# A gated delta-rule layer with experts on one Trainium2 core: solving the right sides twice in place of refining the inverse

## What is computed

```python
mixed = silu(causal_conv4(hidden @ Wqkv.T + bqkv))   # q, k: 8 heads of 128; v: 16 heads of 128
q, k = l2norm(q) * 128 ** -0.5, l2norm(k)            # each used by two value heads
def step(state, inp):                                # state: 16 heads x 128 x 128
    q_t, k_t, v_t, g_t, b_t = inp
    state = state * exp(g_t)
    delta = (v_t - k_t @ state) * b_t
    state = state + outer(k_t, delta)
    return state, q_t @ state
core = rmsnorm(outs) * norm_w * silu(z)
x = x + layernorm(core @ Wout.T + bout)
```

## Time and profile before

| | |
|---|---|
| median of 3 runs | 3361.04 us (3360.9 to 3364.18) |
| span of the profiled execution | 3361.6 us |
| TensorE busy | 3184.6 us, 95% |
| VectorE busy | 2731.3 us, 81% |
| ScalarE busy | 2411.1 us, 72% |
| GpSimd busy | 2147.3 us, 64% |
| DMA queue of the kernel | 15.9% of 16 engines |

### The profile page before, as it was taken

How to read it: one execution, slowest core, us unless ns; L and a number is a source line. 1 busy time by engine, 2 the same in 40 slices (tenths; PEclk the granted TensorE clock), 3 DMA queues, 4 the chain that set the end, 5 groups by cost and what they waited for, 6 DMA issues and landing times.

```text
span 3361.6 us, 77100 instructions
## 1 busy us (share of the span) xinstructions
PE 3184.6 (95%) x23968; PEld 2828.4 (84%) x23968; DVE 2731.3 (81%) x8720; ACT 2411.1 (72%) x5922; POOL 2147.3 (64%) x5380
## 2 busy tenths in 40 slices
PE   4999999999999999999999999999999999999996
PEld 3888888888888888888888888888888888888885
DVE  4788888888888888888888888888888888888874
ACT  3777777777777777777777777777777777777762
POOL 3766666666666666666666666666666666666660
PEclk8999999999999999999999999999999999999997
DMA  4111111111111111111111111111111111111110
GB/s 182 43 40 38 44 40 35 45 41 38 39 45 35 39 47 38 36 45 38 38 45 41 36 37 46 38 39 47 37 35 45 41 38 42 43 35 39 47 36 11
DMA packets 424113, 144.75 MB, mean 43 GB/s; under 512 B 211168, under 2 KB 421664, under 8 KB 423200
## 3 DMA queue, kind: packets, MB, share of 16 engines
q1 hardware_dynamic: 423712, 139.83, 15.9%
HBM read 93.11 MB, written 46.66 MB: 42 GB/s over the span
## 4 chain that ended last, share of the span: by engine, by line
PE 66%; ACT 14%; DVE 5%; issue 5%; POOL 5%; DMA 4%; SPq 0%; ACTq 0%; DVEq 0%; POOLq 0%
PE bF L474 8%; PE bB L648 6%; PE bQ L547 5%; ACT L850 4%; PE bXT L560 4%; PE bB L733 3%; PE bB L720 3%; PE bS L615 3%; PE bD L630 3%; PE bS L623 3%; PE bF L485 3%; PE bS L607 3%; PE bF L487 3%; PE bD L608 2%; PE bX L570 2%
## 5 line engine op out<-in xcount | busy, mean ns | idle before, releaser
L1151 DVE SCALAR_TENSOR_TENSOR Y<-bF,Cv,Y 128x127 f32<-128x127 f32 (+2 forms) x3072 | 852.2, 339 | 8.3 <-ACT Y L867 3.4
L474 PE MATMUL bF<-XnT,Wqkv 128*128 128x128 f32 x4096 | 530.9, 277 | 0.5 <-ACT XnT L986 0.5
L474 PEld LDWEIGHTS bF<-XnT,Wqkv 128*128 128x128 f32 x4096 | 504.4, 193 | 9.3 <-issue 1.8
L867 ACT ACTIVATE Y<-bF,Cv 128x128 f32<-128x128 f32 x1024 | 383.4, 455 | 102.5 <-PE bF L474 102.5
L937 ACT ACTIVATE XiT<-bXT 128x512 fp32r<-128x512 f32 x384 | 229.0, 596 | 298.0 <-PE bXT L560 293.4
L1590 POOL TENSOR_TENSOR Tp<-Tp 32x64 f32<-32x64 f32 (+2 forms) x768 | 362.1, 472 | 60.2
L1194 DVE TENSOR_TENSOR Qi<-bQ,Cf 128x512 fp32r<-128x512 f32 x384 | 262.8, 684 | 98.1 <-PE bQ L547 97.0
L850 ACT ACT_TABLE_LOAD x257 | 329.7, 1283 | 5.4 <-PEq L1674 0.7
L560 PEld LDWEIGHTS bXT<-Qi,Xi 128*128 128x128 f32 x1536 | 221.8, 191 | 118.0 <-issue 88.8
L560 PE MATMUL bXT<-Qi,Xi 128*128 128x128 f32 x1536 | 298.7, 317 | 14.3 <-DVE Qi L1194 2.5
L1583 POOL TENSOR_TENSOR Tp<-Yb,Tm 32x64 f32<-32x64 f32 (+1 forms) x384 | 276.0, 719 | 30.1
(11 more groups left out here) (234 smaller groups left out, 9269.8 us busy)
## 6 DMA issues: line engine op xcount, KB each, us to landing
DL<-Ln SPq DMA_DIRECT2D x128, 256.0 KB, 2.2
XiT<-DX SPq DMA_DIRECT2D x128, 256.0 KB, 2.8
Xi<-DX SPq DMA_DIRECT2D x128, 256.0 KB, 3.2
DX<-Yb SPq DMA_DIRECT2D x256, 32.0 KB, 1.9
...
Cb<-DL SPq DMA_DIRECT2D x128, 32.0 KB, 1.9
...
```

What stands on the lines that cost most here:

```text
L474: last = mm(bank[:, i, :], Wqkv[:, k, c:c + P], XnT[:, k, :], start=(k == 0), stop=(k == KT - 1))
L867: last = op(Y[:, tile, :], bank[:, i, :], ACT.Identity, scale=c[:, TAPS - 1:TAPS], bias=c[:, TAPS:TAPS + 1])
L1151: last = stt(y, bank[:, i, 0:P - shift], Cv[:, g * TILES + tile, n:n + 1], y, ALU.mult, ALU.add)
```

## The change

- The inverse drops the identity product, the third `invert_xt`, `turned`, the fourth mask, the NegR product and the copy into Tt. It gains a third `invert_x`, which ScalarE copies into a new buffer XF in fp32r. XF is used transposed.
- GpSimd subtracts the identity from Ln after the triangle has gone to DRAM (`minus_one`); the first mask has -1 on its diagonal in place of 1.
- The right sides are solved by XF in fp32r (`solve`, from R rounded to Rr by ScalarE), the solution Z goes through Ln in full fp32 (`residual`), VectorE adds R (`left_over`), and `correct` multiplies what is left by XF and adds it to the first solution in bS. ScalarE copies the sum to Z again (`corrected`).
- The state stage runs once for four heads in place of twice for two. R, Z, Qg and Kd double in size; Vs, Kn, AT and Ln are kept for 3 items (`live`), which adds waits ahead of their writers.
- The Xi and XiT loads wait for the last `invert_q` and `invert_x` in place of `correct`. The load of Xr is moved behind them in SyncE's queue.
- The loop over 30 chunks is written out without a loop instruction.
- The orders of the jobs on TensorE, ScalarE and VectorE are new.

```diff
-    f[:, C_LEVEL:C_LEVEL + P] += np.eye(P)
+    f[:, C_LEVEL:C_LEVEL + P] -= np.eye(P)
...
+        def live(w):
+            return (GROUPS * w[0] + w[1]) % LIVE
...
             def inverses_in(f):
                 sp.wait_ge(sem["xs_out"], at("xs_out", f))
                 sp.sem_inc(sem["xs_seen"], 1)
-                sp.wait_ge(sem["c_full"], at("c_full", ahead(f, -1)))
+                sp.wait_ge(sem["q_full"], at("q_full", ahead(f, -1)))
                 sp.dma_start(XiT[:, :, :].bitcast(F32), rows_of(DX[1])).then_inc(sem["xb_in"], 16)
+                sp.wait_ge(sem["x_full"], at("x_full", ahead(f, -1)))
                 sp.dma_start(Xi[:, :, :].bitcast(F32), rows_of(DX[0])).then_inc(sem["xb_in"], 16)
...
                     pe.wait_ge(sem["xb_in"], at("xb_in", v))
-                    mm(bQ[:, :], identb, identb.unsqueeze(1).to_broadcast([P, GH, P]), start=True, stop=True)
                     pe.wait_ge(sem["lnr_done"], at("lnr_done", v))
...
+            def ks(w):
+                t, g = w
+                pe.wait_ge(sem["s_done"], at("s_done", (t - 1, g)))
+                pe.wait_ge(sem["o_done"], at("o_done", ahead(w, -1)))
+                for kh in range(GK):
+                    last = mm(bS[:, 2 * kh * P:2 * (kh + 1) * P], QK[:, g, 2 * kh + 1, :],
+                              S[:, g * GH + 2 * kh:g * GH + 2 * kh + 2, :], start=True, stop=True)
+                last.then_inc(sem["ks_full"], 1)
...
+            def solve(w):
+                pe.wait_ge(sem["xi_done"], at("xi_done", w))
+                pe.wait_ge(sem["rr_done"], at("rr_done", w))
                 for h in range(GH):
+                    last = mm(heads(bS)[:, h, :], XF[:, h, :], Rr[:, h, :], start=(h == 0), stop=True, skip_group_check=True)
+                last.then_inc(sem["z0_full"], 1)
+
+            def residual(w):
+                pe.wait_ge(sem["lni_done"], at("lni_done", w))
+                pe.wait_ge(sem["qg_done"], at("qg_done", w))
+                pe.wait_ge(sem["z0_done"], at("z0_done", w))
                 for h in range(GH):
+                    last = mm(heads(bD)[:, h, :], Ln[:, live(w), h, :], Z[:, h, :], start=True, stop=True)
+                last.then_inc(sem["res_full"], 1)
+
+            def correct(w):
+                pe.wait_ge(sem["res_done"], at("res_done", w))
                 for h in range(GH):
+                    last = mm(heads(bS)[:, h, :], XF[:, h, :], Rr[:, h, :], start=False, stop=True, skip_group_check=True)
                 last.then_inc(sem["zs_full"], 1)
...
+            def rounded_r(w):
+                act.wait_ge(sem["r_done"], at("r_done", w))
+                act.wait_ge(sem["zs_full"], at("zs_full", ahead(w, -1)))
+                op(Rr[:, :, :], R[:, :, :], ACT.Copy).then_inc(sem["rr_done"], 1)
...
+            def left_over(w):
+                dve.wait_ge(sem["res_full"], at("res_full", w))
+                tt(Rr[:, :, :], R[:, :, :], heads(bD), ALU.add).then_inc(sem["res_done"], 1)
...
+            def minus_one(f):
+                pool.wait_ge(sem["neg_done"], at("neg_done", f))
+                pool.wait_ge(sem["ln_out"], at("ln_out", f))
+                tt(Ln[:, live(f), :, :], Ln[:, live(f), :, :], ident.unsqueeze(1).to_broadcast([P, GH, P]), ALU.subtract)\
+                    .then_inc(sem["lni_done"], 1)
```

448 lines of the change are left out of this document (201 added, 247 removed).

## The result

The changed kernel takes **3314.61 us** (median of 4 runs, 3309.96 to 3323.32) against 3361.12 (3360.9 to 3364.18) for the kernel before on the same chip: 0.9863 times, 95% interval 0.9851 to 0.9875. It is faster, but by 46.5 us where the prediction had 167, and 3314.61 lies above its range. The profiled run took 3309.96 us with a span of 3308.2.

The account below looks back on a forecast made before the run. The prediction took TensorE's own instruction time as the bound: 3361.6 less 188 us of TensorE work plus 20 us of moved waits gave 3193.6, stated as 3194 us, with a range of 3115 to 3290.

Parts of the forecast that it names:

- The content of TensorE's queue: TensorE's matmul groups dropped, added and made cheaper: -1.47 us an item, times 128 = -188 us.
- So TensorE's own instruction time sets the pace: Premise from TensorE busy 3184.6 of 3361.6 us: each edit counts by what it takes from TensorE's queue.
- Moved waits: TensorE's waits, mainly on late ScalarE at an item's start: +0.6 us a chunk, +20 us; bounds -70 to +140.
- won back: TensorE waits that go with removed instructions: 1.6 us a chunk gained, set against new losses.
- Rival 1: Whole kernel: TensorE stays the bound and waits come out about even; 3150 to 3245 us, chance 0.56.
- rival 2: TensorE's waits shrink too, with VectorE having 107 us less to do; 3095 to 3150 us, chance 0.15.
- Rival 3: Late PartsT and Z from ScalarE hold TensorE 1.1 to 1.4 us every item; 3245 to 3350 us, chance 0.20.
- Rival 4: GpSimd's uncovered `minus_one` delays each base inverse and Xi and XiT loads by 1.27 us; 3330 to 3367 us, chance 0.04.
- Rival 5: Slower: TensorE's `residual` waits for Z from ScalarE, 2.6 us an item; 3506 us, chance 0.05.
- 1.3 us goes with the shorter item: GpSimd's waiting for Lnk, 2.3 us an item, was to lose 1.3 us.
- The serial chain: An item's steps from state product to O: some 10.5 us against 24 us of item, so it fits if handovers are covered.

Follow-up runs that it names:

- e6: Kernel before with only GpSimd's -1 on the triangle's diagonal brought in and the identity and NegR products dropped; 3351.16 us, ratio 0.9968.
- e7: Kernel before with only Tt and R written in fp32r, so each half of `solve` is two recorded matmuls in place of four; 3337.04 us, ratio 0.9920.
- the four fillers: Useless TensorE matmuls, 0.43 us an item, at the item's end or middle: changed kernel 3340.51 and 3363.82 us, kernel before 3396.18 and 3411.54 us.
- e5: Changed kernel with the first `invert_q` moved ahead of the last projection part on TensorE; 3305.5 us, ratio 0.9833.
- e4: Changed kernel with useless matmuls in TensorE's two gaps of group 0, ahead of `ktr` and the first `invert_xt`; 3283.16 us, ratio 0.9758.
- e3: Changed kernel with GpSimd's `minus_one` cut to 8 columns of one head, for timing only; 3312.31 us, ratio 0.9843.
- e1: Changed kernel with Lnk moved ahead of the query scalings and Rr on ScalarE; 3340.63 us, ratio 0.9921.
- e2: Changed kernel with VectorE's `squares` moved ahead of `right_side`; 3335.78 us, ratio 0.9907.
- h2: Changed kernel with VectorE's two result operations put off behind the squares of the next chunk's group 0; 3309.52 us, ratio 0.9864.

## Why the prediction was wrong

- **The content of TensorE's queue**: -1.47 us an item predicted, -1.43 measured, with the reserve above on how the records split work and waiting. The one unseen shape, `solve` in fp32r with the new operands, has a pitch of 0.48, as taken. From TensorE's timeline of the kernel after:

```profile
1081.61 0.64 PE L597 MATMUL bS<-Rr,XF 128*128 128x128 f32 x4
...
1082.09 0.23 PE L516 MATMUL bXT<-Ch,Parts 128*128 128x128 bf16 x1
```

- **The step that failed first** is the sentence "So TensorE's own instruction time sets the pace, and the question for each edit is what it takes from TensorE's queue". It was drawn from 95% busy. The pace of the kernel after is set by loops that pass through TensorE and ScalarE, in groups 0 and 1 also VectorE, and from group 1 to group 3 TensorE's stretch at the item's end is outside them. e6 (0.09 gained of 0.45 us an item), e7 (0.20 of 0.50) and the four fillers show it. A walk back along releases over 110 us of the steady part gives the shares: before, TensorE 84, ScalarE 18, VectorE 7 us; after, 44, 46 and 18, or up to 52 for TensorE and 33 for ScalarE from another place to start. So of the kernel before the sentence was three quarters true; as its queue was cut, the other paths took over.
- **The term that was mis-sized** is "Moved waits", +0.6 a chunk. It measured +2.9, some 93 us in the run where +20 stood, and its upper bound of +140 covers that. I had the place right (ScalarE late at the start of an item, PartsT and Parts wanted by TensorE: 0.41 + 1.48 us a chunk), but counted each wait as a loss of its own against gains "won back". Two waits I had not named: for the squares' sums behind the experts' result (1.41 a chunk), and for the first mask in group 0 (1.15, with group 1's 1.40), which stands behind `left_over` in VectorE's queue; e5 gave it some 0.8 us more of other matmuls as cover, and the wait stayed.
- **A term that was missing** is the clock: about 0.9 us a chunk. At the run's end, in the window from 3200 to 3300 us the granted clock is 0.73 (0.97 before), but there the kernel after is also nearer to its end. e4 won 31 us by filler alone.
- **Rival 1**, the forecast, fell; so did rival 2, as waits grew. **Rival 3** (ScalarE's lag in each item, 3245 to 3350, with 3313 worked out) holds the result, but only in part for its reason. It wanted 1.1 to 1.4 us more of waiting in every item; idle time grew by 0.7 us an item, with 2.8 and 1.7 us standing in groups 0 and 1 and 0.5 in the others, VectorE was part of the loop there, and the clock gave some of the rest. That its 3313 lies 2 us from the result is luck. **Rival 4**, GpSimd's subtraction, fell by e3; that GpSimd's blocks by way of the transfer of Xi can hold TensorE shows only now and then (5.3 us). **Rival 5** fell: `residual` waited 1.6 us in the whole run.
- Of GpSimd's waiting for Lnk "1.3 us goes with the shorter item": it stayed (295.4 to 296.4 us in all), as Lnk itself comes later.
- The serial chain of "some 10.5 us" does not add up: 1.27, four groups at 0.48 to 0.88, five copies or sums at 0.6 and ten handovers at 0.2 make 8.2 to 9.8. Nothing hung on it.
- **Still open**: what single order of the jobs would take the group 0 and 1 waits away (e1, e2 and h2 took one and fed another, e5 took none); why the end of an item is paid around group 0; what the clock's falls in the run's last 100 us cost; and whether the written-out loop had any part, which wasn't tried apart.
